# A graph layer on one core: sum, norm and gate of each tile moved into the attention loop's last 48 chunks

## What is computed

```python
xn = layernorm(x)
x1 = x + graph_attention(xn, edges) + linear_attention(xn)     # 8 heads; softmax over the edges of each node
h = layernorm(x1)
logits = h @ gate_w + gate_b                                   # 8 experts
idx, prb = argmax(softmax(logits)), max(softmax(logits))
# a row is kept if fewer than C = 977 rows before it, in the order of nodes, chose the same expert
y = (relu(h @ w1[idx] + b1[idx]) @ w2[idx] + b2[idx]) * prb * kept
out = x1 + nan_to_num(y)
```

## Time and profile before

| | us |
|---|---|
| median of 3 runs | 2956.17 (2955.47 to 2956.94) |
| the profiled execution | 2953.88 |
| its span, first to last instruction | 2952.6 |

### The profile page before, as it was taken

How to read it: one execution, slowest core, us unless ns; L and a number is a source line. 1 busy time by engine, 2 the same in 40 slices (tenths; PEclk the granted TensorE clock), 3 DMA queues, 4 the chain that set the end, 5 groups by cost and what they waited for, 6 DMA issues and landing times. The chain is left out here.

```text
span 2952.6 us, 37856 instructions
## 1 busy us (share of the span) xinstructions
PE 2191.0 (74%) x9653; PEld 1727.9 (59%) x9654; DVE 2449.9 (83%) x3309; ACT 1078.0 (37%) x4488; POOL 1974.0 (67%) x1979
## 2 busy tenths in 40 slices
PE   5753777787766777887877767777885655599998
PEld 4551555455555665665666545555664435499988
DVE  5763878888888899999999888899999987566765
ACT  2300211112366666666666411111111114256463
POOL 4175777777777777777777777777777727335453
PEclk9975887888899899989999878999898875599999
DMA  8517888888877777777777788888887735423341
GB/s 249 182 43 156 238 238 239 241 244 247 230 217 218 218 218 218 220 217 218 218 220 217 226 233 248 249 253 253 252 246 223 210 121 171 117 69 82 82 92 15
DMA packets 262373, 579.18 MB, mean 196 GB/s; under 512 B 57174, under 2 KB 141582, under 8 KB 262136
## 3 DMA queue, kind: packets, MB, share of 16 engines
q0 software_dynamic: 151392, 469.80, 57.6%
q1 hardware_dynamic: 101606, 99.38, 10.7%
q10 hardware_dynamic: 9296, 9.05, 0.9%
HBM read 512.54 MB, written 69.78 MB: 197 GB/s over the span
## 5 line engine op out<-in xcount | busy, mean ns | idle before, releaser
L1128 POOL DMA_INDIRECT wide<-kv_d,arena x1099 | 1053.8, 959 | 334.8 <-issue 326.9
L1463 PE MATMUL ps<-wide,arena 128*128 128x264 f32 x2432 | 699.0, 450 | 176.5 <-DVE wide L1566 176.4
L1463 PEld LDWEIGHTS ps<-wide,arena 128*128 128x128 f32 x2432 | 534.4, 225 | 329.4 <-DVE wide L1566 216.7
L1128 POOL DMA_INDIRECT arena<-kv_d,arena x539 | 516.3, 958 | 164.2 <-issue 160.6
L1255 ACT ACTIVATE ps<-wide 128x256 f32 x229 | 88.8, 388 | 1259.0 <-DVE arena L1532 1255.0
L1535 DVE TENSOR_REDUCE arena<-arena 128x64 f32<-128x2048 f32 x229 | 523.4, 2286 | 7.9
L1532 DVE TENSOR_TENSOR arena<-wide,ps 128x2048 f32<-128x2048 f32 x153 | 349.4, 2284 | 114.1 <-DMA wide<-kv_d,arena 113.8
L1463 PE MATMUL ps<-arena 128*128 128x264 f32 x1216 | 338.1, 439 | 88.7 <-DVE arena L1566 88.5
L140 PE MATMUL ps<-halves 128*128 128x256 f32 (+2 forms) x2304 | 360.7, 318 | 2.0 <-DVE halves L1801 2.0
L1566 DVE TENSOR_TENSOR wide<-wide,ps 128x2112 f32<-128x2112 f32 x152 | 356.7, 2347 | 0.0
L1463 PEld LDWEIGHTS ps<-arena 128*128 128x128 f32 x1216 | 259.5, 218 | 160.8 <-DVE arena L1566 108.9
(11 more groups left out here) (348 smaller groups left out, 3255.2 us busy)
## 6 DMA issues: line engine op xcount, KB each, us to landing
wide<-kv_d,arena POOLq DMA_INDIRECT x1099, 3.8
arena<-in_w SPq DMA_DIRECT2D x16, 1024.0 KB, 5.7
kv_d<-wide SPq DMA_DIRECT2D x49, 260.0 KB, 2.4
arena<-xt_d SPq DMA_DIRECT2D x82, 128.0 KB, 3.5
arena<-kv_d,arena POOLq DMA_INDIRECT x539, 3.8
h_d<-wide SPq DMA_DIRECT2D x7, 903.0 KB, 5.1
row_d<-wide SPq DMA_DIRECT2D x7, 896.0 KB, 9.1
xs_d<-wide SPq DMA_DIRECT2D x49, 128.0 KB, 3.6
```

What stands on the lines that cost most here:

```text
L1128: e.indirect_dma_start(out=kvb[k][:, j, :], out_offset=None, in_=kv_d, in_offset=bass.IndirectOffsetOnAxis(ap=ixb[k][:, j:j + 1], axis=0)) ...
L1463: m = e.matmul(psE[(k + 1) % 3][:, 0:264], ident, kvb[b][:, j, 256:ROW], start=(j == 0), stop=(j == J - 1))
```

## The change

Base rows no longer go to DRAM. The auxiliary stage is moved from behind the 12 chunks of M to the end of the loop, and does more. Each chunk has a step; step s gives TensorE tile s-2 to sum (`rows_of`: x + xn M + biases + the attention's output, one PSUM area for all tiles), ScalarE tile s-3 to write to the arena and normalise (`rows_out`), TensorE tile s-4 to turn and tile s-5 to multiply by the gate, and ScalarE the copies of these. SyncE loads a later tile's rows and stores tile s-5's row of h (normalised features, 8 logits, row number; 265 instead of 258 columns). Steps 0 to 47 are in the loop's last 48 chunks, steps 48 to 53 behind it. GpSimd writes x1 of tiles 0 to 45 to `out` behind its last fetch, the last three tiles behind the loop. VectorE forms one-hots and codes at the end of its part of the loop, in two parts (45 and 4 tiles) instead of seven. The probability is formed from the gathered logits in `turn`.

The diff, cut to its core:

```diff
-HW = 258
+HW = 265
-        xm = [R0[:, 8320 + 512 * i:8576 + 512 * i] for i in range(RING)]
-        xr = [R0[:, 8576 + 512 * i:8832 + 512 * i] for i in range(RING)]
+        xm = [R0[:, 8320 + 512 * i:8576 + 512 * i] for i in range(3)]
+        xr = [R0[:, 8576 + 512 * i:8832 + 512 * i] for i in range(3)]
+        hrow = [R0[:, 9856 + HW * i:9856 + HW * (i + 1)] for i in range(3)]
-        base_ps = [ps[4][:, 0:256], ps[7][:, 0:256]]
+        x2_ps, junk = ps[7][:, 0:256], ps[7][:, 256:512]
+        tq_ps, lg_ps = ps[4][:, 0:256], ps[4][:, 256:264]
...
         def rounds(...):
-            between[0]()
-            with turns(aux):
-                for k in range(RING):
-                    body(k, aux=True)
-            between[1]()
             with turns(val(e, cnt_)):
                 for k in range(RING):
                     body(k)
+            between()
+            with turns(AUX - 1):
+                for k in range(RING):
+                    body(k, aux=RING + k)
...
         @block.sync
+            def next_in(i):
+                tile_in(i, val(e, u, 48 * 128))
+                e.reg_add(u, u, 128)
+            def next_out(i):
+                e.dma_start(h_d[bass.ds(val(e, ho, 48 * 128), 128), :], hrow[i]).then_inc(e_hs[i], 16)
+                e.reg_add(ho, ho, 128)
+            for i in range(3):
+                e.nop().then_inc(e_hs[i], 16)
...
+            for t in range(6):
+                if t > 2:
+                    e.wait_ge(e_bp, t - 2)
+                next_in(t % 3)
+            with aligned(e, mybir.EngineType.SP, 14):
+                for i in range(3):
+                    e.reg_add(bw, bw, 1)
+                    e.wait_ge(e_bp, bw)
+                    next_in(i)
+                    e.reg_add(lw, lw, 1)
+                    e.wait_ge(e_lg, lw)
+                    next_out(i)
+            e.wait_ge(e_bp, NT - 3)
+            next_in(0)
+            for t in range(42, NT):
+                e.wait_ge(e_lg, t + 1)
+                next_out(t % 3)
...
         @block.gpsimd
+            for c in range(NT - 3):
+                e.wait_ge(e_bc, c + 2)
+                t_o[0] = s_o.inc(e.indirect_dma_start(out=out, ...qi[:, c, 0:256]...), 16)
...
         @block.scalar
+            def rows_out(i, tile):
+                e.reg_add(bd, bd, 1)
+                e.wait_ge(e_bp, bd)
+                if i == 0:
+                    e.reg_add(hs, hs, 16)
+                e.wait_ge(e_hs[i], hs)
+                link(e.activation(qsf[...tile...], x2_ps, ACT.Identity, accum_out=fs[0]))
+                link(e.activation(fs[1], fs[0], ACT.Copy, scale=-1.0 / 256))
+                link(e.activation(junk, x2_ps, ACT.Square, bias=fs[1], accum_out=fs[2]))
+                link(e.activation(fs[3], fs[2], ACT.Ln, bias=epsc, scale=1.0 / 256))
+                link(e.activation(fs[4], fs[3], ACT.Exp, scale=-0.5))
+                link(e.activation(fs[5], fs[1], ACT.Copy, scale=fs[4]))
+                e.activation(hrow[i][:, 0:256], x2_ps, ACT.Identity, bias=fs[5], scale=fs[4]).then_inc(e_bc, 1)
+                e.activation(hrow[i][:, HW - 1:HW].bitcast(i32), permS[...tile...], ACT.Copy)
+            def turned_out(logits, turn, i, tile):
+                e.reg_add(tq, tq, 1)
+                e.wait_ge(e_tq, tq)
+                if logits:
+                    e.activation(hrow[i][:, 256:264], lg_ps, ACT.Copy)
+                    e.activation(qsf[...tile, 256:264...], lg_ps, ACT.Copy).then_inc(e_lg, 1)
+                if turn:
+                    e.activation(hT, r3(tq_ps, 128), ACT.Copy).then_inc(e_hc, 1)
...
                 tile_end()
-                if aux:
-                    base_out((k - 2) % RING)
+                if aux is not None:
+                    step(aux)
...
         @block.tensor
+            def rows_of(i, tile, written, count):
+                e.reg_add(bp, bp, 1)
+                e.wait_ge(e_x[i], xw)
+                e.wait_ge(e_bc, bp)
+                e.wait_ge(written, count)
+                e.matmul(x2_ps, ident, xr[i], start=True, stop=False)
+                for c in range(2):
+                    e.matmul(x2_ps, xm3[i][:, c, :], M[:, c, :], start=False, stop=False)
+                e.matmul(x2_ps, ones[0:2, :], brow, start=False, stop=False)
+                e.matmul(x2_ps, ident, qsf[...tile...], start=False, stop=True).then_inc(e_bp, 1)
...
                 for j in range(J):
                     m = e.matmul(psE[(k + 1) % 3][:, 0:264], ident, kvb[b][:, j, 256:ROW], start=(j == 0), stop=(j == J - 1))
                 m.then_inc(e_fr, 1)
...
+                if aux is not None:
+                    step_turned(aux)
                 with e.If_eq(f_, 1):
                     project()
-                if aux:
-                    e.wait_ge(e_x[k], xw)
-                    e.wait_ge(e_bc, bp)
-                    base_of(k)
+                if aux is not None:
+                    step_rows(aux)
...
         @block.vector
+            e.wait_ge(e_fr, c6)
+            experts_by_row(e)
...
         def gather(e):
-            wait(G, (t_i0 if e == 0 else t_i1), t_rest if e else None, t_hst[5], t_hst[6], t_hd, ...)
+            wait(G, (t_i0 if e == 0 else t_i1), t_rest if e else None, t_hd, ...)
...
         def turn(e, jj):
             wait(T, t_rl[e][jj])
+            seq(V.tensor_reduce(top_, l, AX.X, ALU.max))
+            t_ = v(V.tensor_tensor(exps, l, top_.unsqueeze(2).to_broadcast([128, 4, 8]), ALU.subtract))
+            wait(S, t_)
+            t_ = a(S.activation(exps, exps, ACT.Exp))
...
+            wait(V, t_)
+            seq(V.tensor_reduce(top_, exps, AX.X, ALU.add))
+            t_pr[e, jj] = v(V.reciprocal(chance[e % 2][:, 4 * jj:4 * jj + 4], top_))
```

More of the change, by code:

```diff
@@ L867, in gps_layer_kernel @@
         s_we = [sem("s_we0"), sem("s_we1")]
[L868 to L879, removed]
+        s_o = sem("s_o")
         cxn, cxT = raw[:, 0:256], r3(raw[:, 256:512], 128)
@@ L956, in aligned, with rounds @@
             return nc.Fori(0, end, engines=(kind,))
-        def rounds(e, pre, body, step, between, aux=AUX, kind=None, before=None):
+        def rounds(e, pre, body, step, between, kind=None, before=None):
             def turns(end, hint=False):
@@ L1197, in tile_end, with link @@
                     e.reg_add(o_at, o_at, QI)
-            def base_out(k):
-                e.reg_add(bc, bc, 1)
-                e.reg_add(bd, bd, 1)
[L1202 to L1206, removed]
+            def link(ins):
+                e.reg_add(fr, fr, 1)
+                ins.then_inc(e_f, 1)
+                e.wait_ge(e_f, fr)
@@ L1353, in _, with turned_of, step_turned, step_rows @@
             m.then_inc(e_fr, 1)
[L1355 to L1361, removed]
+            def rows_of(i, tile, written, count):
+                e.reg_add(bp, bp, 1)
+                if i == 0:
+                    e.reg_add(xw, xw, 32)
+                e.wait_ge(e_x[i], xw)
[5 more added lines that the diff above has]
+                e.matmul(x2_ps, ones[0:2, :], brow, start=False, stop=False)
+                e.matmul(x2_ps, ident, qsf[:, bass.ds(val(e, tile, 48) * QI, 256)], start=False, stop=True).then_inc(e_bp, 1)
+            def turned_of(gate, turn, i):
+                e.reg_add(tq, tq, 1)
+                e.wait_ge(e_hc, tq)
+                if turn:
+                    e.reg_add(hn, hn, 1)
+                    e.wait_ge(e_bc, hn)
+                if gate:
+                    for c in range(2):
+                        e.matmul(lg_ps, hT[:, c, :], gw[:, c, :], start=(c == 0), stop=False)
+                    m = e.matmul(lg_ps, ones[0:1, :], gbias[0:1, :], start=False, stop=True)
+                if turn:
+                    e.transpose(tq_ps[:, 0:128], hrow[i][:, 0:128], ident)
+                    m = e.transpose(tq_ps[:, 128:256], hrow[i][:, 128:256], ident)
+                m.then_inc(e_tq, 1)
+            def step_turned(s_):
+                if s_ >= 4:
+                    turned_of(s_ >= 5, s_ < NT + 4, (s_ - 4) % 3)
+            def step_rows(s_):
+                if 2 <= s_ < NT + 2:
+                    e.reg_add(ao, ao, 1)
+                    rows_of((s_ - 2) % 3, tr, e_ao, ao)
+                    e.reg_add(tr, tr, 1)
             def keys_values(slot, half):
@@ L1875, in gps_layer_kernel @@
-        t_map = carried(6)
-        key = ps[3][:, 0:NT]
-        wait(V, t_map)
+        for c in range(NT - 3, NT):
+            n_ = 128 if c < 48 else N - 48 * 128
+            G.wait_ge(e_bc, c + 2)
+            t_o = s_o.inc(G.indirect_dma_start(out=out, out_offset=bass.IndirectOffsetOnAxis(ap=permS[0:n_, c:c + 1], axis=0),
+                                               in_=qi[0:n_, c, 0:256], in_offset=None), 16)
+        wait(V, t_map[0])
         t = v(V.tensor_tensor(e49(oh_), key.unsqueeze(1).to_broadcast([128, 8, NT]), rev.unsqueeze(2).to_broadcast([128, 8, NT]), ALU.is_equal))
@@ L1987, in gps_layer_kernel @@
         t_hs = {}
[L1988 removed]
+        wait(S, t_bb, t_o, t_rest)
```

422 lines of the change are left out of this document (176 added, 246 removed).

## The result

Before: 2956.17 us. After: **3060.80 us**, median of three runs (3056.26 to 3062.84); the ratio is 1.0351, 95% interval [1.0328, 1.0375]. The forecast was 2969, range 2915 to 3008: the direction was right, the size was not. The profiled execution took 3056.26 (span 3055.0).

What follows compares the result with a forecast made beforehand. VectorE was taken to bound the loop's end, TensorE the experts. The ring delays the loop 86 us, the map comes 14.6 later, about 2 come back: net +13, 2969 us on the median, range 2915 to 3008.

Steps and rivals of the forecast that it cites:

- What bounds the kernel, and what goes: VectorE bounds the loop's end, TensorE the experts; of the 109 us between them, groups and base-row waits leave the path.
- The ring: Last 48 chunks: ScalarE rows 2.55, TensorE product 2.7, SyncE issue 1.4, store landing 3.85, in sequence; 10.5 us against 8.84.
- Member 2: TensorE's rows_of in each step, waiting for ScalarE's rows_out: 2.7 us, priced from the old base product.
- Member 4: Landing of the h store, for which ScalarE's next rows_out waits: 3.8 us plus 0.05 to wake ScalarE.
- Tile-end chunks at 12.0: Chunks in which a tile ends are longer by TensorE's own order: 12.0 us, 11 in the steps that count.
- Step 47: Last step inside the loop: rows_out ends at 2504.0, after 31 steps of 10.5 and 11 of 12.0.
- Steps 48 to 51: Steps behind the loop: 10.5 with SyncE's late store, then 8.2, then 7.1 each without loads, ending at 2536.9.
- Hidden work: VectorE's one-hots and codes, some 18 us, and GpSimd's 46 row writes run beside other work and cost nothing.
- Behind the map, 2 us back: At the experts' start: about 2 us return, as the first expert's fetch no longer waits for an h store.
- Hidden ring: Rival: step stays under 8.84, loop keeps its pace, map 75 us sooner: 2879; chance 0.15 together with the 2.3 landing case.
- The 2.3 us that I rejected: Store landing by the skill page's formula instead of 3.8: step 9.0, time 2916; 4 in 100.
- TensorE as the slower member: Rival: waits bring TensorE's lower clock a third of the time; step 11.1, tile's end 13.5, 38 us more: 3007; chance 0.13.

Runs made afterwards that it cites:

- The kernel with its stage only moved: Kernel before, with its own auxiliary stage of 49 base products moved into the loop's last 48 chunks, nothing else changed: 2959.53 us, ratio 1.0005.
- The store-first run: Changed kernel with SyncE's store of h put ahead of the wait for TensorE's product and the two x loads: 2925.56 us, ratio 0.9891 to the kernel before.

## Why the prediction went wrong, step by step

Everything that follows is from the profiled executions; "ends" are a row's start and duration.

- **What bounds the kernel, and what goes**: right. Of the 120.2 us from the last weighting product to the map 51.9 went.
- **The ring exists, and its four members are those named**: right, and shown: breaking it at one place brought 135 us back, spreading it 145, and TensorE's and SyncE's members, changed alone, each moved the time. ScalarE's and the landing were not changed alone. Of the 41 steps below, the landing releases ScalarE in 30.
- **Member 2, TensorE's product of rows, priced at 2.7**: this is the step that failed. The means of the 41 steps that start from 2064 to 2569 (4, in the last column, is ScalarE's wait for the tile's end and not for the landing):

| member | forecast | measured, 30 steps released by the landing | 11 steps in which a tile ends |
|---|---|---|---|
| 1 ScalarE | 2.55 | 2.79 | 2.81 |
| 2 TensorE | 2.70 | **4.28** | 3.76 |
| 3 SyncE | 1.40 | 1.31 | 1.30 |
| 4 landing and wake | 3.85 | 3.97 | 5.28 |
| step | 10.5 (12.0 where a tile ends) | 12.35 | 13.15 |

At full clock member 2 is 2.9, as forecast and a little more; at the lower level 5.3; between them where the level changes within it. I took the earlier trace rows from a stage in which TensorE kept its clock (granted 0.91 from 1880 to 1990), and moved the price to a stage in which it waits 3 us in front of every product. 1.58 of the 1.85 us that a plain step is longer are this.
- **Member 4**, 3.85: right, 0.12 short. **Member 1**, 2.55: the normalising copy is 0.56, not 0.38. **Member 3**: right.
- **Tile-end chunks at 12.0**: the surcharge is real, and its cause is the forecast's, TensorE's order: ScalarE comes late out of its copy of the output product, 4.8 to 6.2 us after the store was issued in place of 3.97.

```profile
2193.56 0.39 ACT L1289 ACTIVATE wide<-ps 128x256 f32 x1 [6.20 <-PE ps L1605]
2193.87 0.39 ACT L1304 ACTIVATE wide<-ps 128x256 f32 x1
```

Seven of the eleven, with the product at full clock, take 11.8 to 11.9; four, with the lower level, 15.4 to 15.6. So here too the clock is what was missed, 1.15 us a step on average.

- **Step 47**: rows_out ends at 2582.6, forecast 2504.0. 6 us of this were there by step 5 (2052.6 for 2046.5), the rest is 31 plain steps at 1.93 and 11 at 1.15, 72.5 in all.
- **Steps 48 to 51**: forecast 32.9, measured 38.5. Step 49 was to be free of SyncE's loads and cost 8.2; it took 11.4. The others: 11.4 (10.5), 7.4 and 8.3 (7.1 each), the last at the lower clock. **Last gates and map**: 8.4 for 6.4.
- **Hidden work**: right. VectorE starts its one-hots at 2579.14 and then waits 14.7 us for logits. The 46 writes of rows run from 2525.1 to 2595.
- **Behind the map, 2 us back**: not found. The first expert's fetch no longer waits for a store, but the second is held to the end of line 1900, and the stretch is 1.6 longer. The kernel with its stage only moved, in which nothing behind the map was changed, has 425.1 there, so 1 to 2 us say nothing.

```profile
2647.01 2.88 POOL L1943 DMA_INDIRECT arena<-h_d,arena  x1 [12.58 <-DVE arena L1916]
2649.04 5.87 DVE L1900 TENSOR_TENSOR arena<-arena,wide 128x5488 bf16<-128x5488 f32 x1
2650.19 5.56 POOL L1943 DMA_INDIRECT arena<-h_d,arena  x1 [0.30 <-issue]
```

The sum: 78.6 at step 47, 7.6 to the map, 3.6 behind it: 89.8 against 89.6 missed (3056.3 for 2966.7 on the profiled execution).

- **The rivals.** Hidden ring: out, the landing was 3.8 us at the median from 2100 to 2400. The 2.3 us that I rejected came only behind the last fetch of neighbours' rows (2507): from 2500 to 2600 nine stores landed in 2.0 to 3.1, median 2.4, with transfers busy a third of the time in place of 0.6. No run changes the fetches alone, so that they are the reason is not shown. The store-first run shows what a broken ring was worth, 2926, not the 2879 I gave it, because TensorE's product is then still in the way. TensorE as the slower member: this was the true case, and I had undersized it. I gave it the lower clock in a third of the time and 0.6 us a step, although 2.7 us doubled in a third of the steps are 0.9; its 13.5 for a tile's end was near the 13.15 measured. Its last operation but one (line 1496) averages 1.03 us a tile between 2060 and 2500 with 0.69 and 1.22 as its two levels, so about 63%, and the member grew by 1.6 in the plain steps.

What I missed is that the two feed each other. A ring that is too long makes TensorE wait; in the changed kernel the waits lower the granted clock (0.80 for 0.88); this lengthens TensorE's member, so the ring, so the waits. I argued that the busy share "stays near" its old value, 0.7 to 0.8, and it did; the share counts a slow product as more work. The Trainium skill, page "TensorE: Matmul & The Clock Gate", section "HAM oscillation — how this bites in real kernels", describes the first half of this for a kernel whose products wait for a DMA: each wait sends the clock down and the next products run at half rate. The rows agree: 1.22 for 0.70 behind a wait of 3.99, and 36 us back by products that compute nothing. But not every wait did it here: 0.70 stands behind a wait of 1.97.

## What to carry to other kernels

Write down, for a queue that serves two streams, what each wait on it holds back: here a load nobody was waiting for, and the wait for its buffer, stood ahead of a store that everybody was waiting for. Exchanging them was worth 4.4% of the time, 60 of the 135 us by the loads alone. Compare a ring's length with the period of the loop that carries it, and if it is longer, spread the steps before shortening them. And price TensorE's member at both clock levels whenever the change makes TensorE wait.

## What the runs showed that I had not expected

- Work without a use makes a kernel faster where TensorE waits: six products in each of 35 chunks, 36 us; four in each of three steps behind the loop, 8 us.
- A product of 0.7 to 1.2 us, left out at 49 tiles, brought 45 us with the store first (some 40 by the ratios, as the two ran on different chips), 0.8 to 0.9 each; with the ring in place it brought 40 too.
- A store of 132.5 KB lands in 3.8 us while neighbours' rows are being fetched, and in 2.4 behind the last fetch.
